# When TensorE asks for the next unit: in front of its matmuls, or between the last groups of the unit before

## The reference

```python
# --- layer 0 (conv_preact) ---
x = x + _L0_conv_ref(_gn(x), L0_conv_weight, L0_conv_bias)
# --- layer 1 (conv_preact) ---
x = x + _L1_conv_ref(_gn(x), L1_conv_weight, L1_conv_bias)
return x
```

## Time and profile before

| what | value |
|---|---|
| median of 3 runs | 4220.69 us (4217.2 to 4224.03) |
| the profiled execution's own time | 4238.59 us |
| its span from first to last instruction | 4236.8 us |
| mean granted TensorE clock | 0.978 |
| PE busy | 3712.5 us, 88% of the span |
| ACT, POOL, DVE busy | 42%, 32%, 48% |
| DMA | 1435.02 MB, mean 339 GB/s |

### The profile page before, as it was taken

The page is one execution under the profiler, slowest core; times in us unless marked ns, Lnnn a source line. Parts: engine busy times, 40 slices in busy tenths (PEclk is TensorE's granted clock), DMA queues, the critical chain, the costliest instruction groups (busy, mean ns, idle before and its releaser), DMA issues.

```text
span 4236.8 us, 87949 instructions
## 1 busy us (share of the span) xinstructions
PE 3712.5 (88%) x33232; PEld 1551.0 (37%) x33232; DVE 2026.7 (48%) x3110; ACT 1763.8 (42%) x1381; POOL 1363.6 (32%) x1829
## 2 busy tenths in 40 slices
PE   0087877898889999998889999999999999999999
PEld 0032322353333333353333333345564333343333
DVE  6866666565564444445556344444445222332222
ACT  0032222343334555533333555544443555555554
POOL 0011111111113545521111444441211555555555
PEclk9999898999999999999999999999999999999999
DMA  9989999999999999999999999999999999999997
GB/s 323 392 290 392 387 390 380 354 379 379 380 383 303 343 368 379 338 346 381 376 376 351 303 350 368 337 287 373 357 357 317 283 293 288 282 273 292 289 279 226
DMA packets 367108, 1435.02 MB, mean 339 GB/s; under 512 B 49888, under 2 KB 50016, under 8 KB 334176
## 3 DMA queue, kind: packets, MB, share of 16 engines
q10 hardware_dynamic: 176736, 627.30, 48.4%
q0 software_dynamic: 153344, 536.96, 33.5%
q1 hardware_dynamic: 36864, 268.45, 16.9%
HBM read 895.64 MB, written 536.87 MB: 338 GB/s over the span
## 4 chain that ended last, share of the span: by engine, by line
PE 56%; ACTq 12%; issue 12%; DMA 11%; DVE 6%; ACT 1%; POOL 1%; POOLq 0%; DVEq 0%; SPq 0%
PE conv L632 56%; ACTq L479 12%; DMA out_dram<-out_tile 8%; DMA stat_tile<-x_dram 2%; DVE bn_x L681 2%; ACT out_tile L465 1%; DVE out_tile L708 1%; DVE bn_mid L691 1%; POOL x_tile L405 1%; DMA mid_dram<-out_tile 1%; DVE mv_mid L719 1%; POOL out_dram L385 0%; DVEq L681 0%; DVE mv_x L713 0%; POOLq L385 0%
## 5 line engine op out<-in xcount | busy, mean ns | idle before, releaser
L632 PE MATMUL conv<-x_tile,wts 64*64 64x512 f32 x32832 | 3694.7, 600 | 281.2 <-ACT out_tile L465 190.0
L632 PEld LDWEIGHTS conv<-x_tile,wts 64*64 64x64 f32 x32832 | 1530.7, 135 | 2426.2 <-issue 2363.6
L465 ACT ACTIVATE out_tile<-conv,bias 128x1024 f32<-128x1024 f32 x688 | 729.1, 1111 | 1351.2 <-PE conv L632 749.6
L691 DVE BATCH_NORM_STATS2 bn_mid<-out_tile 128x512 f32 (+1 forms) x1376 | 849.5, 680 | 886.1 <-ACT out_tile L465 885.9
L708 DVE TENSOR_SCALAR out_tile<-conv,bias 128x1024 f32<-128x1024 f32 x340 | 436.4, 1283 | 1253.9 <-PE conv L632 1093.9
L371 POOL DMA_DIRECT2D mid_dram<-out_tile x680 | 344.7, 508 | 1712.2 <-ACT out_tile L465 1658.8
L470 ACT ACTIVATE out_tile<-conv,bias 128x1024 f32<-128x1024 f32 x344 | 383.5, 1115 | 831.9 <-PE conv L632 690.0
L508 ACT ACTIVATE x_tile<-x_tile 16x2048 f32<-16x2048 f32 x340 | 648.7, 1908 | 56.7 <-issue 37.4
L681 DVE BATCH_NORM_STATS2 bn_x<-stat_tile 128x512 f32 (+1 forms) x1024 | 629.1, 678 | 49.6 <-DMA stat_tile<-x_dram 49.4
L405 POOL COPY x_tile<-x_tile 16x2048 f32<-16x2048 f32 x340 | 639.8, 1882 | 1.6
L385 POOL DMA_DIRECT2D out_dram<-out_tile x680 | 349.9, 516 | 899.1 <-DVE out_tile L708 830.3
(11 more groups left out here) (62 smaller groups left out, 115.7 us busy)
## 6 DMA issues: line engine op xcount, KB each, us to landing
x_tile<-x_dram ACTq DMA_DIRECT2D x680, 512.0 KB, 22.7
stat_tile<-x_dram SPq DMA_DIRECT2D x256, 1024.0 KB, 9.9
out_dram<-out_tile POOLq DMA_DIRECT2D x680, 384.0 KB, 7.8
mid_dram<-out_tile POOLq DMA_DIRECT2D x672, 384.0 KB, 9.4
x_tile<-mid_dram ACTq DMA_DIRECT2D x340, 640.0 KB, 6.5
x_tile<-mid_dram ACTq DMA_DIRECT2D x344, 128.0 KB, 8.7
mid_dram<-out_tile POOLq DMA_DIRECT2D x8, 416.0 KB, 10.0
x_tile<-x_dram ACTq DMA_DIRECT2D x8, 256.0 KB
```

Source lines behind the costliest of these rows:

```text
L465: last = act.activation(out_tile[0:parts, slot, i], conv[0:parts, bank, i], ACT.Identity, bias=bias0[0:parts, win.parity, int(unit.last), ...
L632: last = nc.tensor.matmul(to, weights, x_tile[HALF * half:HALF * (half + 1), slot, middle, c + kw:c + kw + BANK], start=(kw == 0), stop=(k ...
L691: last = dve.bn_stats(bn_mid[0:parts, unit.win.pair % 2, i, bass.ds(unit.n * 2 + h, 1), :] .rearrange("p a b -> p (a b)"), out_tile[0:part ...
```

## The change

PE's waits for a unit are cut in three and moved forward into the unit before it. wait_for_rows(next) stands ahead of the group c = 512, kw = 0, wait_for_halos(next) ahead of kw = 1, and wait_for_bank(next) ahead of kw = 2. Only the very first unit's rows are asked for in front of it. No other engine's code is changed.

```diff
-            def wait_for_bank(earlier):
+            def wait_for_rows(unit):
+                if unit.win.layer == 0 or unit.last:
+                    pe.wait_ge(x_loaded[unit.slot], (unit.turn + 1) * 32)
+                if unit.win.layer == 1 and unit.kind == TOP:
+                    pe.wait_ge(edge_loaded, 16 * (same_layer_before(unit.win) + 1))
+                if isinstance(unit.n, int) and unit.n < X_RING:
+                    pe.wait_ge(pads_written, unit.win.w * X_RING + unit.n + 1)
+                pe.sem_inc(unit_begun)
+            def wait_for_halos(unit):
+                if unit.win.layer == 1 and unit.kind != TOP:
+                    pe.wait_ge(first_halo, halos_through(unit))
+                if unit.win.layer == 1 and not unit.last:
+                    pe.wait_ge(second_halo, halos_through(unit) + 1)
+                pe.sem_inc(unit_begun)
+            def wait_for_bank(unit):
+                earlier = unit.before(2)
+                if earlier is None:
+                    return
                 pe.wait_ge(evicted_a, earlier.count + 1)
                 if earlier.win.layer == 1:
                     pe.wait_ge(evicted_v, earlier.layer_count + 1)
+                pe.sem_inc(unit_begun)
             def convolve(unit, read=None):
...
-                pe.wait_ge(x_loaded[slot], (unit.turn + 1) * 32)
-                if win.layer == 1:
-                    if unit.kind == TOP:
-                        pe.wait_ge(edge_loaded, 16 * (same_layer_before(win) + 1))
-                    else:
-                        pe.wait_ge(first_halo, halos_through(unit))
-                    if not unit.last:
-                        pe.wait_ge(second_halo, halos_through(unit) + 1)
...
+                following = unit.after(1)
                 for c in range(0, SIDE, BANK):
...
                     for kw in range(KW):
+                        if c and following is not None:
+                            if kw == 0:
+                                wait_for_rows(following)
+                            elif kw == 1:
+                                wait_for_halos(following)
+                            else:
+                                wait_for_bank(following)
```

More of the change, by code:

```diff
@@ L601, in wait_for_bank @@
                     pe.wait_ge(evicted_v, earlier.layer_count + 1)
+                pe.sem_inc(unit_begun)
             def convolve(unit, read=None):
                 win, slot, bank = unit.win, unit.slot, unit.bank
-                pe.wait_ge(x_loaded[slot], (unit.turn + 1) * 32)
-                if win.layer == 1:
-                    if unit.kind == TOP:
-                        pe.wait_ge(edge_loaded, 16 * (same_layer_before(win) + 1))
-                    else:
-                        pe.wait_ge(first_halo, halos_through(unit))
-                    if not unit.last:
-                        pe.wait_ge(second_halo, halos_through(unit) + 1)
-                if isinstance(unit.n, int) and unit.n < X_RING:
-                    pe.wait_ge(pads_written, win.w * X_RING + unit.n + 1)
-                pe.sem_inc(unit_begun)
+                following = unit.after(1)
                 for c in range(0, SIDE, BANK):
@@ L643, in _ @@
             bias_sum(0, 0)
+            wait_for_rows(Unit(WINDOWS[0], 0))
             for win in WINDOWS:
@@ L647, in step @@
                 def step(unit, in_loop):
-                    earlier = unit.before(2)
-                    if earlier is not None:
-                        wait_for_bank(earlier)
                     read = None
```

## The result

| | before | after |
|---|---|---|
| median of the runs | 4220.41 us (4 runs) | 4868.14 us (4 runs, 4865.28 to 4877.74) |
| ratio, 95% interval | 1 | 1.1538 (1.1518 to 1.1558) |
| profiled span | 4236.8 us | 4875.8 us |
| mean granted clock | 0.978 | 0.963 |

A forecast was written before the change was run, and what follows sets the result against it. Layer 1 was taken as bound by eviction, POOL's stores and halo copy, and PE's restart; transfers paced windows 0, 1 and 3. 4238.6 + 564 + 45 = 4848, less 17.9, plus some 10 gave 4840 us, range 4730 to 4970.

The forecast's parts named there:

- The chain of one unit: Layer 1: eviction, copy, PE restart, four rounds, next eviction now span one unit, 7.31 us in loops of windows 6 and 7.
- The sum of layer 1: Four layer 1 windows: 112 units each at 7.31, 7.50 and 7.11 us plus 31 make 2486 us against 1922, +564 us.
- the 31 us: Layer 1: allowance for the four first units and the four short last ones of the windows, 4 x 7.8 us.
- the 4 x 7.8 us: Layer 1: time allowed for the first and short last units, 7.8 us for each of four windows, 31 us together.
- The clock: Layer 1 loop units: stops of some 2 us halve PE's clock in one of 4.5 of 224, 50 falls at 0.9 us, +45 us.
- My bound of 1.3 us for one fall: Layer 1: two or three slow rounds count per clock fall, 0.9 to 1.3 us; at every other stop, at most +218 us.
- Bank and rows at no cost: Moved bank and rows waits were each taken as 0; possible layer 0 costs were at most 56 and 88 us.
- A gain at the restart?: PE's restart after the halo copy, 0.21 to 0.32 us: vanishing entirely would save 84 us; 0 was kept.
- Layer 0: Windows 0, 1, 3 and 5 were to keep 595, 510, 519 and 452 us within 10.
- the zero for the rows wait: Layer 0: asking for x_tile rows 2.6 us earlier costs 0; 88 us if one in ten of 340 units were late.
- The signs: Changed profile: layer 1 windows some 620 us, evictions 7.1 to 7.5 us apart, POOL waits about 600 us, clock about 0.97.
- The rival "faster": Restart of 0.21 us disappears 340 times if the first halo is there at round eight: 4150 us, chance 0.02.

The follow-up runs named there:

- the kernel with the copy in time: Kernel before with rows and bank waits inside the unit before, halo waits in front, POOL's first halo copy ahead of the result wait: 4151.29 us, ratio 0.9853.

## Why the prediction was right, point by point

- **The chain of one unit** was shown. 7.31 us were predicted for loop units of windows 6 and 7, and the timeline has 7.34 in the same three pieces. POOL's piece didn't change with the kernels: 5.09 to 5.10 us in the loops of windows 4, 6 and 7 and 4.78 to 4.79 in straight code, in the kernel before, the changed one and the four experiments that keep the copy behind the stores and the halo wait inside a unit. Moving the wait by two rounds changed the piece behind it by 0.86 us each way (2.87, 2.01, 1.15 us). Undoing the halo wait alone undid the loss.
- **The sum of layer 1.** Predicted +564 and some 10 for late copies, +45 for the clock, 619 in all; the four windows grew by 636.6 us between the starts of their first matmuls. The terms of the size were off both ways. The restart is 0.24 us in the loops of windows 2, 4 and 6 and 0.145 in that of window 7 and in straight code, where I carried over 0.21 to 0.34 and 0.32: where I took 7.50 us for windows 2 and 4 they have 7.29 (5.05 + 0.24 + 2.01) and 7.35 (5.10 for the first piece); window 7 has 7.25 and window 6 7.34 for my 7.31; straight code has 6.94 for 7.11. I had taken these from a place with four kinds of waits and put them at a place with one. That was some 40 us too much. On the other side stand the clock (12 us more than I took), two stops that are long in every window (5.0 us at the loop's exit and 3.4 in its middle, where the others have 2.1: 17 us in the four windows), a stop of 3.4 us in each window's first unit, which the 31 us did not hold (13 us), and the rounding of the windows' borders (3.5 us). 619 - 40 + 12 + 17 + 13 + 3.5 is 625. Of the 12 us that are left some 7 lie in the short last units: from the last eviction of a window to the next window it takes 4.5 us, in the kernel before too, where the 4 x 7.8 us hold 2.6 each (7.8 less 5.2 for the first unit). The last unit has half the matmuls, but its rounds hold two in place of four, so that it still takes twelve. The rest is not divided. Terms that were too high and terms that were too low or missing went against each other, so that the total came within 28 us is in part luck; the mechanism was not.
- **The clock.** 50 falls at 0.9 us were predicted. 50 of 332 units took over 0.2 us longer from restart to eviction than the rest, and the excess over all units is 57 us. That both numbers are so near is luck in part, for the 50 are of several kinds: 8 stand behind the two long stops of each window (3.2 us and more), where the clock fell every time, 41 behind the 216 other loop stops of about 2 us, one in five, and one, in straight code, at full clock; none of the 108 units in straight code, with stops of 1.56 us, had a fall. Window 6, a fall and the unit behind it:

```profile
3757.84 7.08 PE L653 MATMUL conv<-x_tile,wts 64*64 64x512 f32 x48 [1.96 <-POOL x_tile L405]
3766.03 5.38 PE L653 MATMUL conv<-x_tile,wts 64*64 64x512 f32 x48 [1.11 <-POOL x_tile L405]
```

The section of the Trainium skill that the prediction names (TensorE: Matmul & The Clock Gate, "A second HAM failure mode: psum-queue depth-cycling"), read as a fall at every stop, is not borne out at this length. With stops of 2.4 to 3 us (wait at kw = 0) most units have a fall, with regular stops of 1.3 to 1.5 us (wait at kw = 2) none. My bound of 1.3 us for one fall was too low: all four slow rounds behind the wait can count, up to 1.74 us here, and 1.7 to 1.8 us in most of the slowed units with the wait at kw = 0.
- **Bank and rows at no cost** was right in sign and almost in size: together they gain 0.3%. The step that failed is "A gain at the restart? ... No row shows a reason; I keep 0": with the halo waits alone PE restarts 0.06 to 0.2 us sooner. In the changed kernel this is a small part of the whole. And in windows 2 and 4 of the kernel with the copy in time the early bank wait did stop PE, 27 times.
- **Layer 0** was to keep its times within 10 us and did: +5.7 us over four windows. The new waits for loads of x_tile (37.8 us) took the place of waits for the eviction, since the transfers set the pace there. So the zero for the rows wait was right for the time but not in its reason: I took it from the empty list of such waits that the loads are always there six rounds ahead, and 30 times they were not.
- **The signs.** Evictions 7.1 to 7.5 us apart, 608 us of waits on POOL and a clock of 0.96 to 0.97 came as said; the windows were 16 to 21 us longer than the 620 us. Stops over 2.5 us, which I had called a sign of being wrong, do occur, three in each window: in the first unit, in the middle and at the loop's exit.
- **The rival "faster"** needed the copy by round eight, 3.2 us after the eviction began. The kernel in which the first halo is there by then is indeed faster than the kernel before (0.9929), so the point from which it decides was named rightly; only the changed kernel is far from it.

## What to carry to other kernels

Before a wait is moved forward, look at what its releaser hangs on. If the releaser waits for the end of work that is one step back, the old wait lets two steps share the latency, and a wait in the middle of the step makes it the latency of each step, plus everything that stands behind the wait. The new step time can be read from the old trace: the time of the two steps less the work that no longer follows the wait. Then ask whether the releaser needs what it stands behind; here taking the copy forward in POOL's queue gained 1.4 to 1.8%, and made the early wait harmless.

## What the hardware showed that I had not expected

- A stop ended later when other waits stood right behind the one that came last, even if they had been met for microseconds: 0.49 us from the copy's end in the loop with the bank waits behind the halo wait, 0.15 to 0.24 us without them, at the same place of the unit (73 us predicted for the kernel from this, 78 us measured).
- How often the clock fell to 1.2 GHz changed quickly with the length of the stop that comes back in each unit. Behind regular stops of 1.3 to 1.5 us in the loop and of 1.56 us in straight code it never fell, behind those of about 2.0 us it fell at 41 of 216, and with stops of 2.4 to 3 us 237 of 332 units were slowed.
